# Another order in a fused kernel's opening: one batch's output and sum ahead of the next one's exponentials, and four inputs turned earlier

## What is computed

```
x: (8, 256, 128)
layer 0: h = norm(x) * (1 + ca) + sa
         x = x + ga * attention(h)     4 grouped heads of 64, bias by relative position, softmax over 256 keys
         h = norm(x) * (1 + cb) + sb
         x = x + gb * ffn(h)           8 causal heads, each with a gated choice of one expert of 8
layer 1: the same frame around an attention of 16 heads over the heads of one token,
         and a mixture of 8 experts with routing by capacity over all 2048 tokens
```

```python
scores = einsum('bghnd,bhsd->bhns', gq, gk) + gbias
attn = softmax(scores, axis=-1)
out = einsum('bhns,bhsd->bhnd', attn, gv)
out = tile(out.reshape(B, N, KV_HEADS * D_HEAD), (1, 1, G))
return out @ Wo.T
```

## Time and profile before

| | us |
|---|---|
| median of 3 runs | 773.23 |
| the three runs | 774.85, 772.94, 773.23 |
| the profiled execution, device time | 775.72 |
| its span in the profile | 773.8 |
| PE busy in it | 744.0 (96%) |
| DVE busy | 555.0 (72%) |
| ACT busy | 381.5 (49%) |
| POOL busy | 186.7 (24%) |

### The profile page before, as it was taken

One profiled execution on the slowest core, in us unless ns is written; L12 is line 12 of the kernel. 1 busy time (PEld: TensorE's weight loads), 2 busy tenths in 40 slices (PEclk: granted clock), 3 DMA queues, 4 the chain that ended last, 5 costly groups with the idle time before them and its releaser, 6 DMA issues.

```text
span 773.8 us, 16795 instructions
## 1 busy us (share of the span) xinstructions
PE 744.0 (96%) x6559; PEld 563.1 (73%) x6559; DVE 555.0 (72%) x1639; ACT 381.5 (49%) x1059; POOL 186.7 (24%) x233
## 2 busy tenths in 40 slices
PE   7799998999999999999999999999989898999996
PEld 5566756775787578657866876678477777999996
DVE  4887874869676876778677867797949663265986
ACT  3755555356535654564456535633641444544422
POOL 0234221153116301530253035205200421000000
PEclk9999999999999999999999999999999998999999
DMA  8930020402040204020301121021204304000000
GB/s 236 397 93 7 28 56 2 109 1 56 3 109 1 57 2 110 2 55 22 91 19 38 46 67 43 16 68 43 56 2 110 110 17 95 1 1 1 14 22 22
DMA packets 55702, 43.07 MB, mean 56 GB/s; under 512 B 37900, under 2 KB 48804, under 8 KB 54216
## 3 DMA queue, kind: packets, MB, share of 16 engines
q1 hardware_dynamic: 55624, 42.01, 20.4%
HBM read 32.42 MB, written 9.58 MB: 54 GB/s over the span
## 4 chain that ended last, share of the span: by engine, by line
PE 90%; DVE 5%; DMA 2%; issue 1%; POOL 1%; ACT 0%; SPq 0%; DVEq 0%; ACTq 0%
PE ps L1734 15%; PE ps L1813 14%; PE ps L1865 8%; PE ps L2023 6%; PE ps L2001 6%; PE ps L1970 4%; PE ps L1720 4%; PE ps L1742 4%; PE ps L1833 3%; PE ps L1766 3%; PE ps L1755 3%; PE ps L1884 2%; PE ps L1683 2%; PE ps L1656 2%; PE ps L1672 2%; PE ps L1927 2%
## 5 line engine op out<-in xcount | busy, mean ns | idle before, releaser
L1734 PE MATMUL ps<-veF,hB 128*128 128x512 f32 x256 | 121.6, 606 | 0.0
L1289 DVE COPY_PREDICATED shared<-ghot,ps 128x512 f32<-128x512 int32 x128 | 88.3, 727 | 3.1 <-PE ps L1734 0.2
L828 ACT ACTIVATE sc<-sc,nmax 128x128 f32<-128x128 f32 (+1 forms) x128 | 57.2, 447 | 58.7 <-DVE nmax L1275 58.7
L1734 PEld LDWEIGHTS ps<-veF,hB 128*128 128x128 f32 x256 | 45.2, 189 | 49.4 <-issue 39.9
L630 POOL TENSOR_TENSOR sc<-sc,rg 128x384 f32<-128x384 f32 x64 | 51.7, 829 | 69.9 <-DVE rg L1262 69.9
L687 POOL TENSOR_TENSOR ve<-mv,eps 128x2 f32<-128x2 f32 x24 | 8.6, 359 | 241.9 <-DVE mv L1175 241.9
L1865 PE MATMUL ps<-hC,early 128*64 128x128 f32 x1024 | 63.6, 280 | 2.7 <-ACT hC L746 1.6
L1813 PE MATMUL ps<-early_masks,oeF 128*128 128x256 f32 x256 | 62.9, 385 | 1.2 <-issue 1.2
L1865 PEld LDWEIGHTS ps<-hC,early 128*64 128x64 f32 x1024 | 57.3, 140 | 8.3 <-issue 4.6
L1813 PE MATMUL ps<-wide,oeF 128*128 128x256 f32 x256 | 62.5, 386 | 0.0
L2001 PE MATMUL ps<-hE,veF 128*128 128x256 f32 x256 | 58.7, 382 | 0.0
(11 more groups left out here) (252 smaller groups left out, 1535.3 us busy)
## 6 DMA issues: line engine op xcount, KB each, us to landing
chosen<-hot_scratch SPq DMA_DIRECT2D x16, 512.0 KB, 5.8
v_scratch<-shared SPq DMA_DIRECT2D x16, 512.0 KB, 5.2
vg<-v_scratch SPq DMA_DIRECT2D x16, 512.0 KB, 5.6
veF<-in_L_ffn_value_experts SPq DMA_DIRECT2D x1, 2048.0 KB, 9.3
oeF<-in_L_ffn_output_experts SPq DMA_DIRECT2D x1, 2048.0 KB, 14.0
early<-in_L_attn_w_qkv SPq DMA_DIRECT2D x1, 1536.0 KB, 14.5
shared<-bias_scratch SPq DMA_DIRECT2D x2, 512.0 KB, 5.5
veF<-in_L_ffn_W SPq DMA_DIRECT2D x1, 1024.0 KB, 5.3
```

Of the source, the lines that this page charges most:

```text
L828: act.activation(v, v, ACT.Exp, bias=nmax[:, h % RING, t:t + 1], scale=-1.0, accum_out=denB[:, h * T + t:h * T + t + 1]).then_inc(s_("f_e" ...
L1289: dve.copy_predicated(val[:, t, :].rearrange("p (h k) -> p h k", h=HF), ghot[:, t * HF:(t + 1) * HF, e].bitcast(I32).unsqueeze(2) .broadca ...
L1734: pe.matmul(ps[:, vbank(j), :], tok(hB, t), veF[:, :].rearrange("p (h e k) -> p e h k", h=HF, e=EF)[:, e, :, :], start=True, stop=True).th ...
```

## The change

The order of the opening is rearranged. FOLDO is split into SUMO (DVE's sum) and FOLDO (PE's turning and DVE's copy). S1 of batch 1 goes ahead of FOLDO and N0, and ACT's part of it is taken out of it: the exponentials of head 2 (EXP2) come after OUT of batch 0 and those of head 3 (EXP3) after PROJECT. ADD of batch 0 goes ahead of N1 of batch 1. In the first value stage NORMED_LAST goes from "turns" to the "start", directly behind NORMED. The batches 4 and 5 leave TURNED_LAST: PE turns them in "turns" (TURNED_45), behind a wait that all scores of the stage have been read, and ACT writes them in "end" (HELD_45). TURNED_LAST keeps the batches 6 and 7, and its wait on PE is now for DVE's copy of the last turned head.

```diff
-FOLDV, FOLDO, STATS, NORMED, NORMED_LAST, TURNED_NEXT, TURNED_LAST, MOD1, MODDED, KEYS = range(30, 40)
+FOLDV, FOLDO, STATS, NORMED, NORMED_LAST, TURNED_NEXT, TURNED_LAST, MOD1, MODDED, SUMO, EXP2, EXP3, TURNED_45, HELD_45, KEYS = range(30, 45)
...
             attn0(0, 0, T1)
+            opening(0, 0, SUMO)
+            attn0(1, 0, S1)
             opening(0, 0, FOLDO)
             attn0(1, 0, N0)
-            attn0(1, 0, S1)
             attn0(0, 0, V1)
             attn0(0, 0, OUT)
+            attn0(1, 0, EXP2)
             after_attn0(0, 0, PROJECT)
+            attn0(1, 0, EXP3)
             attn0(1, 0, T0)
+            after_attn0(0, 0, ADD)
             attn0(1, 0, N1)
-            after_attn0(0, 0, ADD)
             attn0(1, 0, VP)
...
-                                (opening, 0, 0, {"start": (NORMED,), 2: (TURNED_NEXT,), "turns": (NORMED_LAST,)}),
+                                (opening, 0, 0, {"start": (NORMED, NORMED_LAST), 2: (TURNED_NEXT,), "turns": (TURNED_45,), "end": (HELD_45,)}),
...
-                if n == TURNED_NEXT:
-                    act.wait_ge(s_("h_tr"), 2)
-                    for c in range(AHEAD, 2 * AHEAD):
+                if n in (TURNED_NEXT, HELD_45):
+                    lo = AHEAD if n == TURNED_NEXT else 2 * AHEAD
+                    act.wait_ge(s_("h_tr"), lo // AHEAD + 1)
+                    for c in range(lo, lo + AHEAD):
...
-                if n in (S0, S1):
-                    p = (S0, S1).index(n)
-                    for h in (2 * p, 2 * p + 1):
+                if n in (S0, S1, EXP2, EXP3):
+
+                    heads = {S0: (0, 1), S1: (2, 3) if b != 1 else (), EXP2: (2,), EXP3: (3,)}[n]
+                    for h in heads:
...
+                if n == SUMO:
+                    sum_groups(3)
                 if n == FOLDO:
-                    sum_groups(3)
...
                 if n == TURNED_LAST:
-                    for b in range(2 * AHEAD, B):
+                    for b in range(3 * AHEAD, B):
...
                 if n == TURNED_LAST:
-                    pe.wait_ge(s_("a_sc"), (AHEAD + 1) * 8)
-                    turn_first(2 * AHEAD * T, TILES)
+                    pe.wait_ge(s_("f_pd"), 2)
+                    turn_first(3 * AHEAD * T, TILES)
+                if n == TURNED_45:
+                    pe.wait_ge(s_("f_sc"), 2 * HF)
+                    turn_first(2 * AHEAD * T, 3 * AHEAD * T)
```

## The result

| | median, us | runs | their range | mean clock of the runs |
|---|---|---|---|---|
| before | 773.09 | 4 | 772.30 to 774.85 | - |
| after | 767.62 | 4 | 767.57 to 769.28 | 0.9988 |

The profiled execution of after took 767.65 us with a span of 765.8; that of before took 775.72 with a span of 773.8. The spans differ by 8.0 us.

The account below looks back on a forecast made before the run. PE bounds the kernel, carrying 90% of the chain, with a 3.03 us idle before the projection set by ACT's queue order. 2.65 - 1.57 + 0.44 = 1.5 us off the median gave 771.7 us, range 769.6 to 773.3.

Parts of the forecast that it names:

- Part 1: Opening attention: ACT's copy goes ahead of the exponentials, so the projection starts 2.78 us earlier; the split costs nothing while covered.
- Part 2: After the addition: POOL's division holds DVE's norm passes, so the lead falls from 2.78 to 2.65 us.
- Part 3: First value stage: POOL's long subtraction holds DVE's choice ghot, so PE waits 1.57 us before turning it.
- Rival B: Value stage: ghot is not caught by the long subtraction; gain 3.1 us, 770.1 us; chance 0.22.
- Rival C: Value stage: ghot is caught one operation later, PE starts 3.6 us late; 773.7 us; chance 0.12.
- Part 4: Four input transposes move into PE's 0.93 us hole before the last outputs, gaining 0.44 us in the product stage.
- The sum: Whole kernel: 2.65 - 1.57 + 0.44 = 1.5 us faster, 771.7 us from the median.
- Rival D: Opening: something else holds the projection or the addition, so the change fails to act; some 773.2 us; chance 0.06.

Follow-up runs that it names:

- e1: The kernel before with only the attention steps reordered; POOL's long normalisation and the turning of batches 4 and 5 stay put: 769.44 us, ratio 0.9954.
- e3: The kernel after with POOL's long normalisation cut in two, batches 4 and 5 at place 4, 6 and 7 in "turns": 768.38 us, ratio to before 0.9941.
- e10: e5 again on another chip, the kernel after with three later PE holes filled by idle products: 767.97 us, ratio to before 0.993.
- e11: e8 again on another chip, the kernel before with all four PE holes filled by idle products: 770.85 us, ratio 0.9976.
- e2: The kernel before with only POOL's long normalisation put first and batches 4 and 5 turned beside the first outputs: 773.21 us, ratio 0.9993.
- e4: The kernel before with idle products in three later PE holes, the first hole left open: 771.74 us, ratio 0.9984.
- e7: The kernel before with only the first PE hole, ahead of the first projection, filled by ten idle products: 772.65 us, ratio 0.9989.
- e12: The kernel before with only the first PE hole filled, by eight idle products instead of ten: 771.73 us, ratio 0.9974.
- e5: The kernel after with idle products in the three later PE holes: 767.30 us, ratio to before 0.992.
- e6: The kernel after, unchanged, run again: 770.59 us, ratio to before 0.9974.
- e8: The kernel before with all four PE holes filled by idle products: 770.76 us, ratio 0.9967.

## Why the prediction was wrong

**Part 1** was right: the projection came 2.80 us earlier (3.13 - 0.33) where 2.78 was worked out, at the price of nothing; the split exponentials lay where they were put. The copy of the folded Wo ended at 30.88, before it was wanted.

**Part 2** was right in kind: the norm passes were caught, 1.25 us for both where 1.37 was worked out (36.49 to 37.86), and their turning kept its place (37.36, 3.13 ahead). The loss of 0.13 did not come, as the first pass took 1.00 and not 1.23.

**Part 3** was right: ghot was caught by the long subtraction, 1.55 us long, and PE stood 1.45 us before it. Its lead fell from 3.13 to 1.52, by 1.61 where 1.57 was forecast. Of this 1.26 is the long subtraction. The other 0.35 is lost in e1 too (3.02 to 2.66), where the short subtraction holds the equality for 1.10 us; it belongs to the new order of parts 1 and 2. Rival B, ghot in time, did not come: equality started 0.10 us behind POOL, as put, and was held. Rival C did not come either: L1256 passed between POOL's multiplication and its long subtraction, as the earlier trace rows let one expect, and POOL went on at once. The rule of the Trainium skill, "SBUF — State Buffer", section "Who interferes with whom", that the prediction set against its row did not hold here: L1248 took its 0.23 us at 42.47, inside the root that ran from 41.59 to 43.86. e3 showed the mechanism: with POOL's operation away, the choice took 0.29.

**Part 4** was right: 0.44 us, hidden by the hole, as the lead of 1.95 behind the transposes is 0.43 more than the 1.52 ahead of them.

**The sum** was 1.5 us and came out at 1.6 in the traces, twice: in the leads of after over before (2.80 - 1.61 + 0.43), and between e10 and e11 at 95 us. Rival D is out by both.

**The step that failed** is the last one, from the difference in one trace to the median: "so I take the difference from the median: 771.7". It assumes that everything outside the opening stays as long as it was. The profiled execution of before took 775.72 us with a granted clock of 0.989, and the sum put the clock at nothing without a reason. Three stretches in it at half clock cost 1.7, 1.7 and 2.5 us by the table of leads, nearly four times the forecast gain, and no step says whether after would have them. The row of the page of before that was read as a clock granted in full cannot show this:

```profile
PEclk9999999999999999999999999999999998999999
```

A 9 stands for 90% or more. A slice is 19.3 us, and 3.4 us at half clock in it leave 0.91, which is still a 9; only the stretch of 6.8 us shows, as the 8. The hole of 3.03 us was priced as 3 us of waiting. It has a second price: in e2 and e4 the clock halved at it, and with it filled and nothing moved the median fell by 0.9 us (e7, within the noise) and 1.9 us (e12). The change closes it to 0.74, and so had this second gain.

What the 5.5 us are made of: 1.6 work; by the means over all runs (3.5 us) about 1.9 more, which fits e7 and e12 and goes with a higher clock, 0.9965 in 11 runs against 0.9940 in 80; and 2.0 that only the first four executions had, with next to no half clock, and that is luck as far as the forecast goes. At 0.997 or more stood 8 of 11 executions of after, 9 of 80 of before. An estimate from before's 80 runs alone agrees: a straight line through their times and clocks falls by 0.62 us for each 0.001 of clock, which makes 1.6 of the 3.5 us the clock's and leaves 1.9 for the work and the gaps. The range was too narrow for the same reason. It was drawn around three runs that lay 1.9 us apart, where 80 lie 10 us apart. The mean of 11 runs, 769.8, falls at its low end, and the chance of 0.25 for faster was too small for a change that closes a hole of 3 us.

**What stays open.** The clock's part is not settled closely. e1 also closes the first hole, but its eight runs have a mean clock of 0.9944, no better than before's, though its median is 1.1 us better than its lead of 2.4 explains. Eight to twelve runs of a quantity that jumps by 1.7 us don't tell more. Nor was after run with its first hole opened again and its work left where it is, which would measure the hole's part in the change itself. Why one hole is followed by the low clock in one execution and not in the next was not tested; the two profiles of after differ in it (568 us). The issue gaps, too, are only seen and not explained. A packet of 16 KB of the instruction queue starts 2.3 to 2.6 us before the end of each of the six gaps of e7, e8, e11 and e12, and the next one 1.1 to 1.7 us after it, which suggests the fetching of a program. But each of these profiles has 52 such packets, most of them with no gap beside them; no run tested it.

## What to carry to other kernels

Price a hole of the matrix engine twice: as time, and by whether the clock is full behind it. Read the granted clock in windows of a few us around each long hole, not from slices of 19 us, and take a forecast from one trace to a median only after subtracting stretches at half clock; compare kernels at equal clock. A hole that can't be closed can be filled with products that nobody reads (e5 against e6 on one chip: the median 3.3 us lower, the runs 1.0 us apart instead of 3.6); and POOL's long operations on SBUF belong where DVE has no operation of the same kind that someone waits for (e3).

## What the runs showed of the hardware

- At a single hole of 1.7 to 3.1 us between busy stretches PE's clock can go to 1.2 GHz for 3.4 or 6.8 us, beginning between 0.8 us before the hole's end (e2) and 1.5 us after it (e1), in some executions and not in others. A stretch of 3.4 us cost 1.6 to 1.7 us (before, e4), one of 6.8 cost 2.5 and 2.9 (before, e2).
- The run-to-run spread of this kernel, 768 to 778 us in 80 executions, goes with the mean granted clock (0.997 or more: 768.3 to 771.8; 0.990 or less: 774.8 to 778.4).
- A few added instructions on PE's queue bring or remove gaps of 0.3 to 1.6 us, up to 600 us later, in groups that are the same in both kernels (e7, e8, e11, e12). An edit's effect on a median can't be read below that size without looking for them.
- A DVE operation on SBUF that POOL's 128x512 or 128x1024 holds up ends about 0.15 us after the POOL operation, six times in the timelines of before and after (1.04 beside 1.23 us, 1.95 beside 1.55), and a waiting one gets in between two POOL operations that stand back to back.
